# Handing a softmax normalisation from VectorE to ScalarE and GpSimd in a causal attention block

## What is computed

```python
q, k, v = (qkv[0], qkv[1], qkv[2])
q = _rope(q, positions)
k = _rope(k, positions)
scores = jnp.einsum('bhqd,bhkd->bhqk', q, k) / jnp.sqrt(jnp.float32(dk))
scores = jnp.where(causal[None, None, :, :], scores, -jnp.inf)
attn = jax.nn.softmax(scores, axis=-1)
out = jnp.einsum('bhqk,bhkd->bhqd', attn, v)
...
x = _layernorm(x + _L0_attn_ref(x, L0_attn_W_qkv, L0_attn_W_o), axis=-1)
x = _layernorm(x + _L0_ffn_ref(x, L0_ffn_kernel, L0_ffn_bias, L0_ffn_a, L0_ffn_b), axis=-1)
```

## Time and profile before

| | us |
|---|---|
| median of 3 runs | 443.64 |
| lowest, highest | 441.98, 443.79 |
| the profiled execution | 442.17 |
| its span, first to last instruction | 440.4 |

### The profile page before, as it was taken

The page is one execution under the profiler, slowest core; times in us unless marked ns, Lnnn a source line. Parts: engine busy times, 40 slices in busy tenths (PEclk is TensorE's granted clock), DMA queues, the critical chain, the costliest instruction groups (busy, mean ns, idle before and its releaser), DMA issues.

```text
span 440.4 us, 8586 instructions
## 1 busy us (share of the span) xinstructions
PE 415.8 (94%) x3246; PEld 205.3 (47%) x3246; DVE 379.3 (86%) x491; ACT 317.4 (72%) x643; POOL 119.3 (27%) x188
## 2 busy tenths in 40 slices
PE   5989899799999999999999999999999999999982
PEld 2546445344436353455443644444354454435651
DVE  2878799899999999999999999999987988585585
ACT  2454884386975687777888788878788878898760
POOL 8979602102113100223110322011003012225463
PEclk9999999799999999999999999999999999999996
DMA  7522322210000000022200022200000000000001
GB/s 241 177 97 90 111 81 71 56 30 3 2 0 2 4 1 3 1 80 63 61 3 0 2 66 77 60 3 0 2 1 2 1 3 2 3 25 2 1 26 48
DMA packets 12201, 16.58 MB, mean 38 GB/s; under 512 B 2444, under 2 KB 7324, under 8 KB 12160
## 3 DMA queue, kind: packets, MB, share of 16 engines
q1 hardware_dynamic: 11072, 15.75, 11.3%
q0 software_dynamic: 1088, 0.28, 0.4%
HBM read 10.37 MB, written 5.24 MB: 35 GB/s over the span
## 4 chain that ended last, share of the span: by engine, by line
PE 81%; DVE 8%; ACT 5%; issue 3%; POOL 1%; DMA 1%; POOLq 0%; DVEq 0%; ACTq 0%
PE ps L1289 28%; PE ps L1275 23%; PE ps L1231 17%; DVE pmax L1052 7%; ACT probs L974 4%; PE ps L1199 3%; PE ps L1298 2%; PE ps L1245 1%; PE ps L1241 1%; PE ps L1205 1%; PE ps L1255 1%; PE ps L1317 1%; POOL rstd L856 1%; PE ps L1215 1%; DMA wqkv_sb<-in_L_attn_W_qkv_dram 1%
## 5 line engine op out<-in xcount | busy, mean ns | idle before, releaser
L1052 DVE TENSOR_REDUCE pmax<-ps 128x2 f32<-128x1024 f32 (+3 forms) x273 | 319.2, 1216 | 34.5 <-PE ps L1231 18.7
L974 ACT ACTIVATE probs<-ps 128x512 f32<-128x512 f32 (+2 forms) x576 | 285.4, 583 | 78.1 <-PE ps L1275 76.6
L1275 PE MATMUL ps<-qS,kS 64*128 64x512 f32 (+3 forms) x664 | 163.8, 404 | 2.7 <-DVE pmax L1052 1.3
L1231 PE MATMUL ps<-kS,qS 64*128 64x512 f32 (+3 forms) x640 | 141.9, 414 | 5.5 <-DVE pmax L1052 2.4
L1289 PE MATMUL ps<-probs,vP 128*9 128x512 f32 (+3 forms) x1328 | 144.3, 520 | 0.2
L1275 PEld LDWEIGHTS ps<-qS,kS 64*128 64x128 f32 x664 | 84.5, 186 | 85.5 <-ACT probs L974 61.4
L1231 PEld LDWEIGHTS ps<-kS,qS 64*128 64x128 f32 x640 | 67.1, 185 | 59.8 <-DVE pmax L1052 28.6
L881 POOL TENSOR_SCALAR_AFFINE_SELECT probs<-probs 128x512 f32<-128x512 f32 x64 | 40.3, 635 | 109.7 <-ACT probs L974 109.6
L890 POOL DMA_DIRECT2D qS<-mrows x34 | 19.6, 578 | 167.6 <-DVE mrows L1072 167.4
L1289 PEld LDWEIGHTS ps<-probs,vP 128*9 128x9 f32 x1328 | 22.2, 89 | 42.2 <-issue 24.4
L1245 PEld LDWEIGHTS ps<-causal_x,ident_x 64*128 64x128 f32 x188 | 19.1, 186 | 0.0
(11 more groups left out here) (116 smaller groups left out, 196.1 us busy)
## 6 DMA issues: line engine op xcount, KB each, us to landing
qS<-q_parts SPq DMA_DIRECT2D x52, 64.0 KB
kS<-k_parts SPq DMA_DIRECT2D x52, 64.0 KB
cs<-rope_tables_dram SPq DMA_DIRECT2D x4, 512.0 KB, 6.5
q_parts<-qp SPq DMA_DIRECT2D x4, 512.0 KB, 2.9
k_parts<-kp SPq DMA_DIRECT2D x4, 512.0 KB, 2.8
x_sb<-in_L_attn_x_dram SPq DMA_DIRECT2D x4, 256.0 KB, 5.7
out_dram<-rot SPq DMA_DIRECT2D x2, 256.0 KB, 2.3
qS<-mrows POOLq DMA_DIRECT2D x30, 8.0 KB, 1.8
```

The source lines that it names most:

```text
L974: nc.scalar.activation(probs[:, J % PRING, heads[0]:heads[-1] + 1:2, lo:hi], bank_of(("S", n, j, i))[:, 0:len(heads) * (hi - lo)].rearrang ...
L1052: nc.vector.tensor_reduce(dst, src, AX.X, ALU.max).then_inc(unit_free, 1)
L1231: last = nc.tensor.matmul(ps[:, HELD[e][hl], at:at + w], qS[rows, b, c, hp, ii * TOK:(ii + 1) * TOK], kS[rows, b, kk, hp, 0:w], start=i == ...
L1275: last = nc.tensor.matmul(bank_of(("S", n, j, i))[:, x * w:(x + 1) * w], kS[rows, b, j // TPC, hp, (j % TPC) * TOK:(j % TPC + 1) * TOK], q ...
```

## The change

For the tasks of groups 0, 1 and 2 (0 to 11) the turn's bank is no longer read by VectorE. ScalarE copies its 4 tiles x 4 heads x 9 columns into a new buffer `sums` of two halves (`copy_sums`) and frees the bank. GpSimd raises the column of sums to the power -1 and multiplies (`normalise` on GpSimd, two instructions with a wait between), both at the event's place in the common list. Before each it waits for the copy, ScalarE for the half to be free. Tasks 12 to 16 are normalised by VectorE as before. GpSimd fills a small buffer with -1 in its opening. TensorE waits for the normalisation of task 11 before it transposes the first chunk's result.

The planner's costs for `O` change with it: for these tasks ScalarE is booked 0.27 and VectorE nothing; GpSimd is booked nothing. With other costs the search gives another list.

```diff
         elif kind == "O":
             g, c, first, end = TASKS[e[0]]
-            self.aside(0.55 * (end - first) / TPC, 0.6, ready)
+            if g < NG - 1:
+                self.act = max(self.act, self.whole(0.55, ready) + self.TO_ACT) + 0.27
+                self.side = (self.side[0] + 0.55, self.side[1])
+                self.give(self.act + self.TO_PE, self.took)
+            else:
+                self.aside(0.55 * (end - first) / TPC, 0.6, ready)
...
+        inverse = sb("inverse", [128, TPC, HG, 1])
+        minus = sb("minus", [128, TPC, HG, 1])
+        sums = sb("sums", [128, 2, TPC, HG, VC])
...
-            if copied_by_act(e):
+            if e[0] == "O" and TASKS[e[1]][0] < NG - 1:
+                RELEASE[e] = (o_copied, e[1] + 1)
+            elif copied_by_act(e):
...
+            pool.memset(minus[:, :, :, :], -1.0).then_inc(half_set, 1)
...
+            def normalise(n):
+                g, c, first, end = TASKS[n]
+                pool.wait_ge(o_copied, n + 1)
+                of = sums[:, n % 2, first:end, :, :]
+                to = on[:, c * TPC + first:c * TPC + end, g * HG * DK:(g + 1) * HG * DK].rearrange("p t (h d) -> p t h d", d=DK)
+                pool.wait_ge(half_set, 2)
+                if n > 0:
+                    pool.wait_ge(o_normed, n)
+                pool.tensor_tensor(inverse[:, first:end, :, :], of[:, :, :, DK:VC], minus[:, first:end, :, :], ALU.pow).then_inc(inverted, 1)
+                pool.wait_ge(inverted, n + 1)
+                pool.tensor_tensor(to, of[:, :, :, 0:DK], inverse[:, first:end, :, :].to_broadcast([128, end - first, HG, DK]), ALU.mult).then_inc(o_normed, 1)
...
+            def copy_sums(n):
+                e, (g, c, first, end), (lo, hi) = ("O", n), TASKS[n], queries(n)
+                act.wait_ge(unit_done, UNIT[e])
+                if n >= 2:
+                    act.wait_ge(o_normed, n - 1)
+                o = bank_of(e)[:, lo:hi].rearrange("p (t h r) -> p t h r", t=end - first, r=VW)
+                nc.scalar.copy(sums[:, n % 2, first:end, :, :], o[:, :, :, 0:VC]).then_inc(o_copied, 1)
...
-                if e[0] == "O":
+                if e[0] == "O" and TASKS[e[1]][0] == NG - 1:
                     normalise(e[1])
...
                 if k == 2:
                     released(pe, ("O", n))
+                    pe.wait_ge(o_normed, LAST_OF[NG - 2] + 1)
```

More of the change, by code:

```diff
@@ L606, in attention_block @@
         unit_done = sem("unit_done")
+        inverted = sem("inverted")
+        o_copied = sem("o_copied")
+        o_normed = sem("o_normed")
         unit_free = sem("unit_free")
@@ L901, in _ @@
                     load_maxima(e[1])
+                if e[0] == "O" and TASKS[e[1]][0] < NG - 1:
+                    normalise(e[1])
                 if e[0] == "P" and e[1] >= COPIED:
@@ L990, in _ @@
             for e in SCHEDULE:
+                if e[0] == "O" and TASKS[e[1]][0] < NG - 1:
+                    copy_sums(e[1])
                 if copied_by_act(e):
@@ L1094, in normalise @@
                 dve.wait_ge(unit_done, UNIT[e])
-                if n > 0:
+                if n > LAST_OF[NG - 2] + 1:
                     released(dve, ("O", n - 1))
@@ L1098, in normalise @@
                 nc.vector.reciprocal(rsum[:, first:end, :], o[:, :, :, DK]).then_inc(rs_done, 1)
-                dve.wait_ge(rs_done, n + 1)
+                dve.wait_ge(rs_done, n - LAST_OF[NG - 2])
                 nc.vector.tensor_tensor(on[:, c * TPC + first:c * TPC + end, g * HG * DK:(g + 1) * HG * DK].rearrange("p t (h d) -> p t h d", d=DK),
```

## The result

The changed kernel took **448.32 us** (median of 4 runs, 447.51 to 454.97); the kernel before, on the same chip, 443.01 (4 runs, 441.98 to 443.79). The ratio is **1.0115, 95% interval 1.0076 to 1.0154**: slower by 1.2%, over twice the 0.5% that a measurement can tell. The prediction was 442.2 us and its range ended at 447.0, so both the sign and the range were wrong. (The 454.97 is one execution at a mean granted clock of 0.954.) The profiled execution took 447.51 us, against 442.17 before; TensorE's mean granted clock is nearly the same in both, 0.983 and 0.984.

The account below looks back on a forecast made before the run. TensorE, 81% of the chain, was taken as the bound. -1.5 - 0.4 - 2.5 - 1.0 + 0.4 (ScalarE's copies) + 1.0 + 2.6 = -1.4 us against the 443.64 median gave 442.2 us, range 438.2 to 447.0.

Parts of the forecast that it names:

- the size and place of the new work: Per turn of tasks 0 to 11: ScalarE copy 0.30 us; GpSimd power 3.0 and product 0.44 us.
- The case of a cheap GpSimd: Rival: GpSimd's power stays at 1.04 us whatever the count, stalls 0 and 0.6 us; 439.2 us, chance 0.06.
- the stalls: TensorE waits for masks of tasks 5 and 8 behind GpSimd's normalisation of tasks 4 and 7: +1.0 and +2.6 us.
- the other ten, a little under half, -2.5: Normalisations other than tasks 1 and 3: taking each off VectorE saves 0.25 us, -2.5 in all, ends 0 and -5.4.
- task 3, -0.4: Task 3's normalisation at 145 us, standing on the chain: its removal from VectorE saves 0.4 us.
- task 1, -1.5: Between task 1's turn and task 2's first product: VectorE's relief and one reduction fewer save 1.5 us net.
- the clock, -1.0: Low clock in 84 to 88 us: a shorter poor stretch of TensorE may avoid it, even odds, -1.0, ends 0 and -2.1.
- VectorE's idle time before reductions growing by less than 3 us up to 340: Sign: growth under 3 us up to 340 us expected; growth by all 6.5 would mean the ten brought nothing.
- Wrong if the time before 60 us differs: Sign: the forecast is wrong altogether if time before 60 us differs, since nothing in that stretch was moved.
- The slower case: Rival: masks of tasks 5 and 8 late behind GpSimd's normalisation, the ten and the clock bring nothing; 446.7 us, chance 0.24.
- No change: Rival: TensorE's chain hides the ten normalisations, the clock falls as before, stalls of 1.5 us; 443.6 us, chance 0.18.
- The full relief: Rival: all VectorE's 1.9 + 5.4 us and the clock's 2.1 gained, less added costs, -5.0; 438.6 us, chance 0.12.

Follow-up runs that it names:

- The old order with nothing but the relief: Changed kernel run in the old list of events, with tasks 4 and 7 normalised behind the masks of tasks 5 and 8: 442.96 us, ratio 0.9993.
- both calls moved: Changed kernel, same list, GpSimd normalising tasks 4 and 7 only behind the last masks of tasks 5 and 8: 444.37 us, ratio 1.0014; repeated, 444.1 us, 1.001.
- the last set: Changed kernel with neither, task 4's, task 7's or both normalisations behind the next task's masks, in five rounds: 449.37, 447.8, 445.76, 444.1 us.
- the kernel before at a width of 210: Kernel before with the planner's search keeping 210 courses instead of 200, so another list: 443.16 us, ratio 0.9998.

## Why the prediction was wrong

**Right: the size and place of the new work.** Power, product and copy came within 8% of their estimates, the slope of two rows on 2 and 4 elements held at 16 (2.93 us), and both waits on GpSimd were there, where and as often as the text said.

The Trainium skill, GPSIMD Engine Reference, section Engine selection, has an elementwise add, product or maximum of two inputs at about twice VectorE's time. The trace has 1.4 times for the product (0.408 us on GpSimd, 0.292 on VectorE for 128 elements), less than the rule. The section doesn't name a power, and the rule can't be carried over to it: 2.933 us against 0.248 of VectorE's reciprocal is twelve times. The case of a cheap GpSimd failed on that.

**Nearly right: the stalls.** The terms were +1.0 and +2.6, from 5.8 less 4.8 us and 6.9 less 4.3; measured 5.4 less 4.3 and 6.5 less 4.4. Sum 3.2, 3.6 forecast. They were taken whole, and that was right: the 2.2 us between the turns of tasks 7 and 13 are the whole of the second wait.

**Wrong: "the other ten, a little under half, -2.5".** This is the step that failed: it let VectorE's relief count where TensorE hardly waits for VectorE. The old order with nothing but the relief gave 0.9993 [0.996, 1.0026], and within it the lead of 0.07 us at 93 us had become a lag of 0.43 at 341: nothing for these turns. The argument was that VectorE is busy 37.91 of 40 us, so that what delays one engine delays both. But the row beside it in the same line says 39.90 of 40 for TensorE: with 0.1 us idle there, there was nothing for VectorE to give. TensorE waited for reductions 3.7 us in the whole kernel, most of it at task 1. The bound at the bottom, 0, was the right one, and the line already contained it.

**Wrong: task 3, -0.4.** It stood on the chain with 0.4 us. With the relief in the old order the turn of task 3 comes at 143.21 instead of 143.09 and that of task 4 at 186.13 instead of 186.20, so at most 0.2 us is gained between, and none of it is kept. A piece of VectorE on the chain shows that it ended last, not by how much.

**Too large: task 1, -1.5.** The gap of 5.2 us fell to 2.7, 2.5 us less; but with the old order and the same relief only 1.0 us is kept at 93 us. What the new order adds at this place wasn't measured alone. The gap between two named instructions isn't the time of the program.

**Half right: the clock, -1.0.** The poor stretch did get better in the stall-free new order: its 80 to 84 us has clock 1.00, and over its twelve runs the mean granted clock is 0.983, against 0.977 of the nineteen runs of the kernel before beside them. But falls came elsewhere, which the text had not looked for, as the profile of the kernel with both calls moved shows in the second of two stretches:

```profile
80.00:84.00 4.00, 3.08 (x17) 1.17 (x17) 4.00 (x5) 3.05 (x7) 2.03 (x2) 1.00 0.32 93
...
140.00:150.00 10.00, 8.30 (x50) 3.42 (x48) 8.12 (x11) 5.40 (x11) 5.26 (x6) 0.83 0.03 5
```

In the changed kernel nothing was left of the gain. Its six runs in the last set have 0.974, and its first profile has 0.79 in each of 48 to 56, 80 to 88 and 144 to 152 us, where the kernel before has 1.00, 0.61 and 1.00.

All twelve profiles of the searched-anew list have a clock below 1 between 142 and 154 us; the kernel before, the same with its transposes doubled and both kernels with the old list and the new work have 1.00 there. But the kernel before at a width of 210 has such a fall too (0.88 in 148 to 154) and its median is no higher for it, so this fall alone is not shown to take the gain away.

The new order has a cost of its own, and where it arises is open. Executions at a like clock show it: at 0.980 those with both calls moved took 444.88 and 444.98 us, those of the kernel before in the same set 442.03 to 443.03. In the profiles, from task 0's turn to task 13's, both take 343.4 us, although the kernel before has a clock of 0.61 in 80 to 88 us and 0.96 in 88 to 96 and the other only the one fall, 0.79 in 144 to 152. So at an equal clock the new order costs some 2 us even with the relief, and its higher clock hides most of it; with both calls moved only 0.5 us of loss is left in the medians. This is an estimate: a run's mean clock doesn't say where it fell. The prediction had no term for such a cost.

The last set then reads: 449.37 less 443.64 is 5.7 us, of which 1.1 + 2.1 are the waits, 0.5 stay with both calls moved, and 2.1, known to about 2, go for the most part with the lower clock of the changed kernel.

**The checks.** Both waits, the power's time, the 2.7 us gap: as stated. "VectorE's idle time before reductions growing by less than 3 us up to 340" was met too, 23.3 to 25.5, and it misled: by 340 us the new list has put 243 reductions instead of 240, 2.8 us of work, in the place of idle time. In the old order with the relief, with 240 as before, it is 27.0. The 3.7 us more are most of the relief turned into idle time. "Wrong if the time before 60 us differs": it does, by a clock of 0.88 in 46 to 60 us where the kernel before had 1.00. No instruction of TensorE moved there, and such a fall comes and goes with the same list: the old order with the new work has one, the kernel before has none, and with both calls moved there is none either. The test was badly chosen.

**The rivals.** The slower case (446.7, chance 0.24) was nearest to the truth, in mechanism, places and condition: that the ten turns bring nothing, and the clock nothing in this kernel. Its power of 3.5 us was not needed; with 2.93 the waits were 3.2 instead of 4.6 us, and the lower clock, which it lacked, more than made up for that: 448.32 is 1.6 us above it. "No change" held for the relief alone. The full relief adds up to -4.6 by its own terms, not to the -5.0 that was written; that changed no chance.

The fault lay in weighing. Two terms that no row carried, -2.5 and -1.0, turned a sum of +2.1 into -1.4. That is not all of it: +2.1 is still 3.2 short of the 5.3 measured. Of the -1.9 for tasks 1 and 3 at most 1.0 was seen, and the cost of the new order and the clock behind the stall had no term.

## What to carry to other kernels

Take work off an engine only where the profile shows the bounding engine waiting for it: TensorE idle 2 of 248 us, and waiting 3.7 us for reductions in all, is about the most that VectorE's relief could give here, whatever VectorE's own share. Before long work goes to an engine that is mostly idle, look at what short, urgent work is queued behind it; 2.9 us in front of a 0.64 us mask cost 1.1 and 2.1 us here, and issuing it behind the masks took both waits away. And measure order and assignment apart, since a searched order can lean on the assignment: here it cost 2.1% without it.

## What the runs showed that was not expected

- **The power on GpSimd is dear by element**: 0.74, 1.04 and 2.93 us for 2, 4 and 16 elements a partition, where the product of 16 takes 0.23.
- **The clock makes the spread.** Executions of one kernel differ with their mean granted clock: before 442.01 us at 0.984 to 448.25 at 0.961, changed kernel 446.23 at 0.990 to 452.14 at 0.964. Compare kernels at a like clock as well as by their medians: here the two give 3 to 4 and 5.3 us for the same pair. Behind the stall at task 8 the clock fell in three of five profiled executions, in one with 1.5 us on top of 2.1, and in none of the eleven without a stall there.
- **Neither busy engine's time counts in full.** On the 86% busy VectorE 6.5 us more cost 2.1 us, and 6.5 less gave nothing that could be told; on the 94% busy TensorE 5.2 us more in the profile cost 4.2.
